# Two image rows per turn of the main loop on TensorE, ScalarE and VectorE

## What is computed

```python
x = x + involution7x7(ln_c(x))      # per-pixel 7x7 kernels, from two 1x1 convolutions
t = tokens(x);  t = t + moe(ln_t(t))        # 16 experts, top 2 by softmax
x = x + conv3x3_lowrank(ln_c(x))    # folds into one 3x3 convolution
t = tokens(x);  t = t + lstm(ln_t(t))       # over 56*56 = 3136 tokens in order
```

```python
i = sigmoid(xi + h @ V_i);  g = tanh(xg + h @ V_c);  o = sigmoid(xo + h @ V_o)
c = h * c + i * g
h = o * tanh(c)
```

## Time and profile before

| | |
|---|---|
| median of 3 runs | 4271.69 us (4267.42 to 4274.11) |
| profiled execution | 4263.86 us |
| its span | 4262.1 us |
| mean granted TensorE clock | 0.529 |
| first step of the recurrence (L576) | 331.0 us |
| last one | 4256.7 us |
| a turn of the main loop | 70.07 us (961.93 to 1032.00) |

### The profile page before, as it was taken

The page is one execution under the profiler, slowest core; times in us unless marked ns, Lnnn a source line. Parts: engine busy times, 40 slices in busy tenths (PEclk is TensorE's granted clock), DMA queues, the critical chain, the costliest instruction groups (busy, mean ns, idle before and its releaser), DMA issues.

```text
span 4262.1 us, 135780 instructions
## 1 busy us (share of the span) xinstructions
PE 3681.5 (86%) x35548; PEld 2444.0 (57%) x35548; DVE 3419.6 (80%) x21767; ACT 2647.1 (62%) x11685; POOL 2250.8 (53%) x3306
## 2 busy tenths in 40 slices
PE   3678989898989989898989898989898989888887
PEld 2455655555565656565656565656555555655555
DVE  3337888888888888888888888888888888887777
ACT  1326666666666666666666666666666666665665
POOL 5765555555555555555555555555555555552222
PEclk9875555555555555555555555555555555555555
DMA  4000000000000000000000000000000000000000
GB/s 69 1 1 2 1 1 1 1 1 1 1 1 1 1 1 1 1 1 1 1 1 1 1 1 1 1 1 1 1 1 1 1 1 1 1 1 2 1 1 1
DMA packets 44543, 11.09 MB, mean 3 GB/s; under 512 B 39913, under 2 KB 44010, under 8 KB 44490
## 3 DMA queue, kind: packets, MB, share of 16 engines
q1 hardware_dynamic: 42378, 10.05, 1.5%
q10 hardware_dynamic: 2112, 0.46, 0.1%
HBM read 7.29 MB, written 3.21 MB: 2 GB/s over the span
## 4 chain that ended last, share of the span: by engine, by line
PE 55%; ACT 18%; DVE 17%; issue 7%; POOL 3%; SPq 0%; POOLq 0%; DVEq 0%; DMA 0%; ACTq 0%
PE GATES L1076 22%; ACT O L579 9%; PE YB L912 8%; ACT G L576 8%; DVE HR L740 8%; DVE O L737 7%; PE TAPB L899 5%; PE YB L1043 5%; PE DB L1011 5%; PE DB L893 3%; PE H1B L935 2%; PE H2B L935 1%; PE TAPB L940 1%; POOL ACC L427 1%; PE TAPB L1052 1%
## 5 line engine op out<-in xcount | busy, mean ns | idle before, releaser
L576 ACT ACTIVATE G<-GATES 128x12 f32<-128x12 f32 x3136 | 571.1, 182 | 1256.2 <-PE GATES L1076 1199.8
L1076 PEld LDWEIGHTS GATES<-HR,VN 128*128 128x128 f16 x9408 | 494.9, 108 | 1303.2 <-DVE HR L740 1249.7
L1076 PE MATMUL GATES<-HR,VN 128*128 128x4 f16 x9408 | 757.6, 175 | 390.8 <-DVE HR L740 255.3
L732 DVE TENSOR_TENSOR_SCAN CT<-G,CT 128x12 f32<-128x12 f32 x3136 | 586.7, 187 | 305.4 <-ACT G L576 265.7
L579 ACT ACTIVATE O<-G 128x16 f32<-128x16 f32 x3136 | 688.5, 220 | 98.6 <-ACT G L576 0.2
L737 DVE RECIPROCAL O<-O 128x4 f32<-128x4 f32 x3136 | 570.0, 182 | 196.8 <-ACT O L579 0.9
L1076 PE MATMUL GATES<-H,VW 128*128 128x4 f16 x9408 | 714.2, 170 | 0.0
L409 POOL TENSOR_TENSOR HD<-VV,DBS 128x448 f32<-128x448 f32 x420 | 475.4, 1132 | 272.4 <-ACT DBS L568 272.4
L740 DVE TENSOR_TENSOR_SCAN HR<-O,CT 128x20 f16<-128x20 f32 x3136 | 613.2, 196 | 4.5
L401 POOL TENSOR_TENSOR PA<-PA,XN 128x336 f32<-128x336 f32 x392 | 328.6, 838 | 536.2 <-ACT PA L535 536.0
L749 DVE SCALAR_TENSOR_TENSOR CT<-HIST,CT 128x4 f32<-128x4 f32 x3136 | 522.9, 167 | 108.9
(11 more groups left out here) (204 smaller groups left out, 5604.7 us busy)
## 6 DMA issues: line engine op xcount, KB each, us to landing
out_dram<-OUT SPq DMA_DIRECT2D x112, 28.0 KB, 2.0
X<-in_x_dram SPq DMA_DIRECT2D x4, 672.0 KB, 12.5
STG<-in_L_ffn_w_dram SPq DMA_DIRECT2D x4, 512.0 KB, 8.3
U<-in_L_conv_U2s_dram SPq DMA_DIRECT2D x1, 972.0 KB
W<-in_L_ffn_w_dram SPq DMA_DIRECT2D x1, 512.0 KB, 11.5
X<-in_x_dram ACTq DMA_DIRECT2D x4, 112.0 KB, 3.0
S<-in_L_conv_S1s_dram SPq DMA_DIRECT2D x1, 108.0 KB
S<-in_L_conv_S2s_dram SPq DMA_DIRECT2D x1, 108.0 KB
```

The source lines that it names most:

```text
L576: act.activation(G6[:, :, 2:5], gates[c][:, w, :, :], ACT.Tanh, scale=1 / GSCALE).then_inc(step_in, 1)
L732: dve.tensor_tensor_scan(CELL.rearrange("z b k -> z (b k)"), G6[:, :, :].rearrange("z b k -> z (b k)")[:, 0::2], ADD3.rearrange("z b k -> ...
L1076: last = pe.matmul(gates[c][:, w, :, SLOT[g]], wt[:, g].rearrange("z m c -> z (m c)"), digit, start=False, stop=True, skip_group_check=True)
```

## The change

On ScalarE, VectorE and TensorE the main loop has 25 turns instead of 50, and its body holds two rows, `j = 2 i` and `j = 2 i + 1`, one behind the other. GpSimd's and SyncE's loops stay. All other loops stay too.

```diff
@@ ScalarE
-            with rows(act, LAG, H) as j:
-                act_row(act, j, True, True, True, True)
+            with rows(act, LAG // 2, H // 2) as i:
+                for u in range(2):
+                    act_row(act, 2 * i + u, True, True, True, True)
@@ VectorE
-            with rows(dve, LAG, H) as j:
-                dve_row(dve, j, True, True, True, True)
+            with rows(dve, LAG // 2, H // 2) as i:
+                for u in range(2):
+                    dve_row(dve, 2 * i + u, True, True, True, True)
@@ TensorE
-            with rows(pe, LAG, H) as j:
-                pe_row(pe, j, True, True, True, True)
+            with rows(pe, LAG // 2, H // 2) as i:
+                for u in range(2):
+                    pe_row(pe, 2 * i + u, True, True, True, True)
```

## The result

| | before | changed |
|---|---|---|
| median of 5 runs | 4267.86 us (4264.67 to 4274.11) | 4286.34 us (4283.42 to 4291.83) |
| profiled execution | 4263.86 us | 4291.83 us |
| its span | 4262.1 us | 4288.9 us |

The changed kernel is slower: ratio 1.0043, 95% interval 1.0028 to 1.0058 (12 to 25 us), and by 18.5 us in the medians. A second measurement gave 1.0046 (1.0030 to 1.0061).

What follows compares the result with a forecast made beforehand. The prediction took the recurrence, 56 chained steps per row, as the bound. Branches removed (-2.0) and code reloaded (+44.4) summed to +42.4 us, 4314 us against the median 4271.69, range 4265 to 4357.

Steps and rivals of the forecast that it cites:

- Bound by the recurrence: Main loop: 56 chained steps per row, 1.25 us each; only what lengthens a step lengthens the kernel.
- Term 1: Main-loop back edges: 25 fewer on each engine, worth 0.08 us each on VectorE only, -2.0 us.
- the 13 register entries: VectorE's other entries saved per pair of rows, register work between steps: taken as 0, 9 us if on the chain.
- Term 2: Doubled main-loop bodies don't stay in the buffers: 14 q14 pieces reloaded each turn at 0.127 us, +44.4 us.
- Term 3: Main-loop jump back: the hint brings the first piece in time, at one request's price, already among the 14.
- First rival: Main loop: buffers hold the doubled body or requests are hidden; only the branch goes, 4269.7 us; chance 0.17.
- Second rival: Main-loop back edge: the branch waits 3.22 us a turn for its first piece, 77 us more, 4391 us; chance 0.15.
- Signs named: Main loop: 14 q14 and 11 q8 packets every turn; pair 141.9 us; seam step 1.25 us; some eight steps delayed.

Runs made afterwards that it cites:

- TensorE alone: Two rows per turn on TensorE only, one on ScalarE and VectorE, against the kernel before: ratio 0.9994, on repeat 0.9996.
- VectorE alone: Two rows per turn on VectorE only, old loop on the other engines, against the kernel before: ratio 1.0038, median +16.7 us.
- other slots: Changed kernel with main-loop bodies begun 31 (VectorE) and 32 (ScalarE) entries into a piece: 1.0054 to before; third choice, 30 and 83: 1.0023.

## Why the prediction was right or wrong

The direction, the mechanism and the range held; the size did not: +42.4 us forecast, +18.5 measured. (Of the distance between the forecast 4314 us and the measured 4286, 3.8 us are the median of before, 4267.86 against the 4271.69 that I started from.)

- **Bound by the recurrence:** right. Every delay on the chain shows in the time at its full size, and the sums of steps give the medians within 5 us.
- **Term 1, branches removed, -2.0 us:** right in size. The seam (step 56) is 0.07 us shorter, x 25 = 1.9 us. I took 0 for the 13 register entries (12 by the traces' records), with the reason that their steps are not late by the profile. That reading was not complete: steps 2, 8 and 10 take 1.30, 1.29 and 1.28 us before. Steps 2 and 58 are 0.05 us shorter each, 2.5 us in all, in the kernel with TensorE alone too (step 58 also with VectorE alone). But step 2 is as short in the run without hints on TensorE and ScalarE, whose bodies are otherwise unchanged, and in the first turn before (1.25 us). So fewer register entries don't explain step 2; its cause is open.
- **Term 2, doubled bodies are loaded each turn:** the mechanism is right to the packet: 14 on q14 and 11 on q8 were forecast and counted. **The step that failed is its price, "0.127 us each", times 14.** The 14 pieces cost 0.86 us a turn, 0.061 each, 21.5 us instead of 44.4. I had the price from three requests a turn in the first turns of two loops, and wrote that the 14 places would be "spread over 112 steps much as those were". They weren't the same lot: in the main loop's first turn two of three stood at L737 and L579, where steps 15 and 20 were 0.22 and 0.18 us longer; the third, at L747, cost nothing. Both places return in the changed kernel, at 0.20 and 0.13 us, but among 14 they are two. Only five of the 14 cost anything. I had even seen that some requests fall in slack, and could have counted: the order of the instructions says with which entry each piece begins, so the forecast could have priced 14 named places instead of a mean. It would still have lacked the price of the back edge, and of a place such as step 57 under other slots.
- **Term 3, the back edge's request among the 14:** too small at 0.127 us. It costs 0.29 us more than the old back edge, the dearest of this kernel's requests.
- **First rival (fits, or requests hidden):** false on size, as the 14 and 11 packets a turn show, and false on the time: 18.5 us more, not 2.0 less. Nine of 14 requests on VectorE and ScalarE and all 11 on TensorE cost nothing. Its -2.0 us was a little nearer to the measured +18.5 than my +42.4; the five requests that aren't hidden make the loss.
- **Second rival (the branch waits):** false with the hint, true without it (+2.8 us a back edge). In the changed kernel's trace the hint at 2026.26 us stands 140.6 us ahead of its branch at 2166.87.
- **Signs named:** packets as forecast; a pair of 141.9 us was forecast, and it is 140.8 (141.13 less the 0.38 of that execution); delays at "some eight steps", and there are five, one of them at L745, which I hadn't named. The step behind the seam is at 1.25 us, as forecast. The last loop's first turn shows its 4 packets on q8 again, and its entry takes 4.15 us, not 4.47.

## What to carry to other kernels

A loop of a chain-bound kernel should fit its engine's instruction buffer (on VectorE four pieces of 128 entries were held and five not), counted from the slot at which it begins; unrolling past that traded a branch of 0.08 us for requests of up to 0.3 us each, most of which cost nothing here. Which ones hit seems to be a matter of slack in the sequencer, and no rule for it was shown, so it has to be measured. If a body can't fit, moving it by some entries moves the requests: here that alone made 9 us of 15 pieces a turn and 23 us of 14. And where a body just fills the buffer, as VectorE's four pieces did, keep the hint on its closing branch: leaving it out cost 133 us, more than everything else tried here.

## What was not expected of the hardware

- The hint guards a body that is entirely resident. Without it VectorE's four-piece body was loaded anew in every turn (5 packets, 2.89 us idle); with it never in the 49 turns behind the first. Leaving it out had one good side: in the changed kernel the jump out of the loop found its code there (a step of 1.25 us instead of 4.15, once; the step behind it took 1.80 us). In the kernel before without it that step took 3.74 us instead of 4.47, as ScalarE stood 2.88 us for "issue".
- A request for a piece can hold up the engine that makes it: by 0.24 us on VectorE (L738 at 0.49 us instead of 0.25), by 0.16 on ScalarE (L579 at 0.37 instead of 0.21). On TensorE 11 requests a turn cost nothing.
- Executions differ as a whole by 0.1 to 0.2 us a row: the unchanged last loop took 69.93 to 70.13 us in the profiles of this study. Comparing two profiled spans without that control would have put the loss at 27 us instead of 18.5.
